# Layer norm statistics of the attention output: ScalarE sums and squares with GpSimd, in place of VectorE's batch-norm instructions

## What is computed

```python
attn = jax.nn.softmax(A1, axis=-1) - lamb * jax.nn.softmax(A2, axis=-1)
out = jnp.einsum('bhqk,bhkd->bhqd', attn, V)
out = out.transpose(0, 2, 1, 3).reshape(B, S, DIM)
out = out @ Wo
mu = jnp.mean(out, axis=-1, keepdims=True)
var = jnp.var(out, axis=-1, keepdims=True)
out = (out - mu) * jax.lax.rsqrt(var + LN_EPS) * gamma + beta
```

## Time and profile before

| what | value |
|---|---|
| median of 3 runs | 3935.44 us (3934.48 to 3940.17) |
| the profiled execution | 3935.01 us |
| its span, first to last instruction | 3933.2 us |
| mean granted TensorE clock | 0.981 of full speed |
| TensorE busy | 3720.3 us (95%) |
| VectorE busy | 3152.2 us (80%) |
| ScalarE busy | 2786.4 us (71%) |
| GpSimd busy | 1550.2 us (39%) |

### The profile page before, as it was taken

How to read it: one execution, slowest core, us unless ns; L and a number is a source line. 1 busy time by engine, 2 the same in 40 slices (tenths; PEclk the granted TensorE clock), 3 DMA queues, 4 the chain that set the end, 5 groups by cost and what they waited for, 6 DMA issues and landing times. The chain is left out here.

```text
span 3933.2 us, 63904 instructions
## 1 busy us (share of the span) xinstructions
PE 3720.3 (95%) x23714; PEld 1464.6 (37%) x23714; DVE 3152.2 (80%) x5433; ACT 2786.4 (71%) x3257; POOL 1550.2 (39%) x2057
## 2 busy tenths in 40 slices
PE   7997999999999999999999999999999879899999
PEld 5664222222222222222222222222222245588888
DVE  6776899999989999998999999899999433345454
ACT  4343888888888888887888788888888946522221
POOL 2320353263235325333532543253344357763330
PEclk9998999999999999999999999999999989899999
DMA  8775111111111111111101111110112069732220
GB/s 298 269 265 186 33 39 42 50 33 34 58 33 39 34 57 33 34 52 34 44 28 52 39 39 33 47 49 28 44 38 83 33 237 327 231 118 87 74 86 22
DMA packets 224553, 330.85 MB, mean 84 GB/s; under 512 B 29281, under 2 KB 165092, under 8 KB 219636
## 3 DMA queue, kind: packets, MB, share of 16 engines
q1 hardware_dynamic: 205812, 276.40, 21.3%
q0 software_dynamic: 18432, 50.36, 3.8%
HBM read 169.27 MB, written 156.34 MB: 83 GB/s over the span
## 5 line engine op out<-in xcount | busy, mean ns | idle before, releaser
L1734 DVE TENSOR_REDUCE first_rows<-psum 128x1 f32<-128x512 f32 x4000 | 2509.4, 684 | 173.1 <-PE psum L185 157.5
L1579 ACT ACTIVATE arena<-psum,exp_scale 128x1024 f32<-128x1024 f32 x2048 | 2159.8, 1111 | 275.8 <-PE psum L1439 269.8
L1455 PE MATMUL psum<-arena 128*32 128x512 f32 x8200 | 1107.5, 612 | 1.2 <-ACT arena L1579 0.6
L1619 POOL TENSOR_TENSOR arena<-arena 128x16 f32<-128x16 f32 x129 | 376.9, 2922 | 1504.0 <-ACT arena L1545 1504.0
L185 PE MATMUL psum<-arena 48*128 48x512 f16 x2048 | 649.6, 391 | 51.1 <-DVE first_rows L1734 22.8
L185 PE MATMUL psum<-first_rows 48*128 48x512 f16 x2048 | 622.7, 386 | 36.7 <-ACT arena L1539 7.7
L185 PEld LDWEIGHTS psum<-arena 48*128 48x128 f16 x2048 | 157.8, 93 | 865.2 <-DVE first_rows L1734 721.1
L185 PEld LDWEIGHTS psum<-first_rows 48*128 48x128 f16 x2048 | 154.9, 92 | 836.8 <-DVE first_rows L1734 715.1
L1439 PE MATMUL psum<-arena 50*128 50x512 f16 x2048 | 444.8, 382 | 11.6 <-ACT arena L1579 8.5
L1439 PE MATMUL psum<-first_rows 50*128 50x512 f16 x2048 | 447.3, 384 | 6.9 <-DMA first_rows<-arena 3.0
L1136 ACT ACTIVATE mix_arena<-psum,mix_arena 128x1024 f32<-128x1024 f32 x64 | 71.4, 1115 | 327.1 <-DVE mix_arena L1156 327.1
(11 more groups left out here) (186 smaller groups left out, 3944.0 us busy)
## 6 DMA issues: line engine op xcount, KB each, us to landing
scratch_split<-route_arena SPq DMA_DIRECT2D x64, 512.0 KB, 3.2
scratch_sorted_x<-route_arena SPq DMA_DIRECT2D x60, 512.0 KB, 4.7
scratch_sorted_y<-leaf_arena SPq DMA_DIRECT2D x60, 512.0 KB, 3.9
first_rows<-scratch_split SPq DMA_DIRECT2D x384, 64.0 KB, 2.2
arena<-scratch_split SPq DMA_DIRECT2D x384, 64.0 KB, 2.2
leaf_arena<-scratch_sorted_x SPq DMA_DIRECT2D x44, 512.0 KB, 5.8
leaf_start<-in_leafw SPq DMA_DIRECT2D x2, 5128.0 KB, 17.6
arena<-in_x SPq DMA_DIRECT2D x18, 512.0 KB, 4.9
```

The lines of the kernel that those rows point to most:

```text
L1455: last = nc.tensor.matmul(value_bank[32 * j:32 * j + 32, :], vaug[:, batch % 2, kt, 2 * pair + j % 2, :], prob[:, step % 2, j, :], start=k ...
L1579: nc.scalar.activation(prob[:, step % 2, 2 * h:2 * h + 2, :], score[:, 2 * h:2 * h + 2, :], ACT.Exp, scale=exp_scale[:, s % 2, s // 2:s // ...
L1619: nc.gpsimd.tensor_tensor(linv[:, c], total, minus_one, ALU.pow).then_inc(ochain, 1)
L1734: nc.vector.tensor_reduce(halfmax[:, odd, 2 * m + h, qt, c:c + 1], aux_bank[bank], AX.X, ALU.max).then_inc(bank_used[bank], 1)
```

## The change

The projections are read with an identity that also sums each row. GpSimd makes the negative mean of it (`mean`), in set 0 for group 0 and in set 1 for group 1. ScalarE squares the centred rows with a sum (`square`), one tile at the end of each of the steps 1 to 4 of set 1 (group 0) and set 2 (group 1); the squares themselves go to a buffer that is free by then. GpSimd makes the variance from the sum at the head of `inverse_std`, and `finish` adds the negative mean. VectorE's statistics go away.

```diff
--- before.py
+++ after.py
@@ -1588,6 +1588,8 @@
                                 act.wait_ge(extra_full, extras_before(k) + 1)
                                 read(i, s, kind, number, k % AUX)
                             k += 1
+                        if s in (1, 2) and 1 <= step <= OutputGroup.G:
+                            groups[s - 1].square(nc, act, i, step - 1)
 
             for i in range(BATCH):
                 body(i, i == LAST)
@@ -1599,6 +1601,9 @@
                     read_o(1, BATCH * 2 * PER_BATCH, k % AUX)
                 else:
                     read_group(BATCH, kind, number, k % AUX)
+            for h in range(2):
+                for q in range(OutputGroup.G):
+                    groups[h].square(nc, act, BATCH, q)
 
         @block.gpsimd
         def _(pool):
@@ -1672,6 +1677,9 @@
                         pool.wait_ge(extra_full, extras_before(group_end(i, 0, "turn")) + 1)
                     wait_read(pool, place(i, s, 11, "o", 0))
                     join_maps(2 * n + 1, s, 0)
+                    if s in (0, 1):
+                        wait_read(pool, group_end(i, s, "out"))
+                        groups[s].mean(nc)
                     if s in (1, 2):
                         groups[s - 1].inverse_std(nc, pool, i)
                         groups[s - 1].finish(nc, pool, nc.gpsimd, i)
@@ -1689,6 +1697,9 @@
                 body(i, i == LAST)
             wait_read(pool, START[BATCH] + EPILOGUE.index(("o", 1)))
             join_maps(BATCH * 2 * PER_BATCH, PER_BATCH - 1, 1)
+            for h in range(2):
+                wait_read(pool, START[BATCH] + EPILOGUE.index((f"out{h}", 3)))
+                groups[h].mean(nc)
             for h in range(2):
                 groups[h].inverse_std(nc, pool, BATCH)
 
@@ -1758,16 +1769,9 @@
                                     wait_read(dve, k)
                                     join_max(target % 2, i * PER_BATCH + target)
                             k += 1
-                        for h in range(2):
-                            if (s, step) == (1, 1 if h == 0 else 14):
-                                wait_read(dve, group_end(i, h, "out"))
-                                groups[h].stats(nc, link)
 
             for i in range(BATCH):
                 body(i, i == LAST)
-            for h in range(2):
-                wait_read(dve, START[BATCH] + EPILOGUE.index((f"out{h}", 3)))
-                groups[h].stats(nc, link)
             for h in range(2):
                 groups[h].finish(nc, dve, nc.vector, BATCH)
 
@@ -1792,7 +1796,7 @@
 
     G = 4
     LINKS = 2
-    POOL_LINKS = 9
+    POOL_LINKS = 10
 
     def __init__(self, nc, ctx, ar, consts, prefix):
         G = self.G
@@ -1800,15 +1804,14 @@
         self.sum_in = ar.take(G, DIM)
         self.oT = ar.take(G, KC, P)
         self.y = ar.take(G, DIM)
-        self.bn = ar.take(G, 6)
-        self.mv = ar.take(G, 2)
+        self.total, self.nmean, self.squares = ar.take(G), ar.take(G), ar.take(G)
         self.var, self.power, self.rstd, self.tmp = ar.take(G), ar.take(G), ar.take(G), ar.take(G)
 
         def sem(name):
             return ctx.enter_context(nc.semaphore(prefix + name))
 
         self.sum_ready, self.stored = sem("sum_ready"), sem("stored")
-        self.var_ready = sem("var_ready")
+        self.nmean_ready, self.squared = sem("nmean_ready"), sem("squared")
         self.pchain, self.y_ready = sem("group_pchain"), sem("y_ready")
 
     def tokens(self, a, g):
@@ -1839,44 +1842,47 @@
         return nc.scalar.activation(self.oT[:, 2 * q:2 * q + 2].rearrange("p q a b -> p (q a b)"), bank, ACT.Copy)
 
     def read_projected(self, nc, bank, q):
-        return nc.scalar.activation(self.y[:, q], bank[:, 0:DIM], ACT.Copy)
-
-    def stats(self, nc, link):
-        for q in range(self.G):
-            ins = nc.vector.bn_stats(self.bn[:, q], self.y[:, q])
-        link(ins)
-        for q in range(self.G):
-            ins = nc.vector.bn_aggr(self.mv[:, q], self.bn[:, q])
-        link(ins)
-        nc.vector.tensor_scalar(self.var, self.mv[:, :, 1], LN_EPS, None, ALU.add).then_inc(self.var_ready, 1)
+        return nc.scalar.activation(self.y[:, q], bank[:, 0:DIM], ACT.Identity, accum_out=self.total[:, q:q + 1])
+
+    def square(self, nc, act, n, q):
+
+        act.wait_ge(self.nmean_ready, n + 1)
+        nc.scalar.activation(self.oT[:, q].rearrange("p a b -> p (a b)"), self.y[:, q], ACT.Square, bias=self.nmean[:, q:q + 1],
+                             accum_out=self.squares[:, q:q + 1]).then_inc(self.squared, 1)
+
+    def mean(self, nc):
+
+        nc.gpsimd.tensor_scalar(self.nmean, self.total, -1.0 / DIM, None, ALU.mult).then_inc(self.nmean_ready, 1)
 
     def inverse_std(self, nc, pool, n):
 
         done = n * self.POOL_LINKS
-        pool.wait_ge(self.var_ready, n + 1)
+        pool.wait_ge(self.squared, (n + 1) * self.G)
+        nc.gpsimd.tensor_scalar(self.var, self.squares, 1.0 / DIM, LN_EPS, ALU.mult, ALU.add).then_inc(self.pchain, 1)
+        pool.wait_ge(self.pchain, done + 1)
         nc.gpsimd.tensor_tensor(self.rstd, self.var, self.power, ALU.pow).then_inc(self.pchain, 1)
-        pool.wait_ge(self.pchain, done + 1)
+        pool.wait_ge(self.pchain, done + 2)
         nc.gpsimd.tensor_tensor(self.tmp, self.rstd, self.rstd, ALU.mult).then_inc(self.pchain, 1)
-        pool.wait_ge(self.pchain, done + 2)
+        pool.wait_ge(self.pchain, done + 3)
         nc.gpsimd.tensor_tensor(self.tmp, self.tmp, self.var, ALU.mult).then_inc(self.pchain, 1)
-        pool.wait_ge(self.pchain, done + 3)
+        pool.wait_ge(self.pchain, done + 4)
         nc.gpsimd.tensor_scalar(self.tmp, self.tmp, -0.5, 1.5, ALU.mult, ALU.add).then_inc(self.pchain, 1)
-        pool.wait_ge(self.pchain, done + 4)
+        pool.wait_ge(self.pchain, done + 5)
         nc.gpsimd.tensor_tensor(self.rstd, self.rstd, self.tmp, ALU.mult).then_inc(self.pchain, 1)
 
     def finish(self, nc, eng, ops, n):
 
         done = n * self.POOL_LINKS
         wide = [P, self.G, DIM]
-        eng.wait_ge(self.pchain, done + 5)
-        ops.tensor_tensor(self.y, self.y, self.mv[:, :, 0:1].to_broadcast(wide), ALU.subtract).then_inc(self.pchain, 1)
         eng.wait_ge(self.pchain, done + 6)
+        ops.tensor_tensor(self.y, self.y, self.nmean.unsqueeze(2).to_broadcast(wide), ALU.add).then_inc(self.pchain, 1)
+        eng.wait_ge(self.pchain, done + 7)
         ops.tensor_tensor(self.y, self.y, self.rstd.unsqueeze(2).to_broadcast(wide), ALU.mult).then_inc(self.pchain, 1)
-        eng.wait_ge(self.pchain, done + 7)
+        eng.wait_ge(self.pchain, done + 8)
         ops.tensor_tensor(self.y, self.y, self.consts.gamma.unsqueeze(1).to_broadcast(wide), ALU.mult).then_inc(self.pchain, 1)
-        eng.wait_ge(self.pchain, done + 8)
+        eng.wait_ge(self.pchain, done + 9)
         ops.tensor_tensor(self.y, self.y, self.consts.beta.unsqueeze(1).to_broadcast(wide), ALU.add).then_inc(self.pchain, 1)
-        eng.wait_ge(self.pchain, done + 9)
+        eng.wait_ge(self.pchain, done + 10)
         eng.wait_ge(self.sum_ready, n * 16 + 16)
         ops.tensor_tensor(self.y, self.y, self.sum_in, ALU.add).then_inc(self.y_ready, 1)
 
```

## The result

The changed kernel takes 3885.62 us (median of 4 runs, 3881.76 to 3886.74) where the kernel before takes 3935.35 (4 runs, 3934.48 to 3940.17): a ratio of 0.9874 [0.9862, 0.9887], 1.26% faster, 49.7 us less. The forecast was 3895.5: the right direction, and 9.9 us too little, just outside the lower end of the range.

The account below looks back on a forecast made before the run. The prediction took VectorE's row maxima to bound the attention stage, with the statistics standing in VectorE's queue. Its sum: 3935.4 - 50.4 + 6.4 + 0 + 0 + 4.1 = 3895.5 us, range 3886 to 3922.

Parts of the forecast that it names:

- The statistics, -50.4: Attention loop: without VectorE's statistics the 16 three-step windows fall to plain steps, -50.4 us; at the least -29.3.
- its first rival: Loop: the stall goes, but TensorE still runs at 1.2 GHz there; only 29.3 us come back, 3917 us; chance 0.06.
- 21.1 us: Loop: the part of the statistics' 50.4 us put down to TensorE's slow clock behind the stall.
- The accumulator read in the projection, +6.4: Loop's projection steps: ScalarE's extra read releases the bank 0.10 us later, lengthening each step: +6.4 us, between 0 and 18.
- the ring: Projection step: projection, ScalarE's read, then TensorE's row product waiting for that read; a release 0.10 us later lengthens it by 0.10.
- The end of the stage, +4.1: End of attention: last squares, GpSimd's longer chain and the finishes are not hidden, +4.1 us, between +2.9 and +6.
- The squares, 0: Loop, four steps per group: ScalarE's 2.58 us in a 2.49 us step is covered by idle time: 0, at most 13 us.
- GpSimd, 0: Loop: a mean per group and one more inverse-deviation operation, about 0.3 us each, hold up nothing: 0.
- Another function table: Square steps: squares lie in another table, two loads for every square, +170 us, about 4070 us; chance 0.04.
- The clock part stays: Loop: ScalarE's backlog leaves TensorE short pauses and the 1.2 GHz clock; only 29.3 us come back, 3917 us; chance 0.06.
- Nothing changes: Loop: some other wait fills the same place, for example exponentials behind a late mean; about 3938 us; chance 0.04.
- ScalarE becomes the bound: Square and projection steps: nothing overlaps in square steps and accumulator reads cost their whole length; 3922 us; chance 0.10.

Follow-up runs that it names:

- Experiment 1: The kernel before without VectorE's statistics inside the loop and nothing in their place (groups there normalised with mean 0, variance 1): 3881.75 us, 0.9869.
- experiment 2: The changed kernel with VectorE's statistics put back at their two places in the loop, result not used: 3938.83 us, 1.0018.
- experiment 3: The kernel before with each group's statistics left on VectorE but spread over five steps, one tile per step: 3901.97 us, 0.9921.
- Experiments 4 and 5: The changed kernel with an unused copy behind each projection read, which then releases the bank: 64 columns (4), 3891.26 us; 256 columns (5), 3902.18 us.
- experiment 6: The changed kernel with every square inside the loop made twice, the second into a spare buffer: 3904.46 us, 0.993.
- experiment 7: The changed kernel with VectorE making mean and variance again in the epilogue, in place of the squares there: 3882.69 us, 0.9875.

## Why the prediction was right or wrong

**The statistics, -50.4: right**, in sum and in parts. The 16 windows fell to 119.74 us. Experiment 1 removes nothing else and gets -50.7 in the loop (2766.39 to 2715.72); experiment 2 puts the statistics back and loses the gain. That the slow clock goes with the pause, which the forecast assumed and its first rival doubted, is shown from the other side by experiment 3. That the sum was hit within 0.3 us is in part luck: where the clock falls differs from one execution to the next (experiment 2), and the forecast took its 21.1 us from the very execution that it is compared with.

**The accumulator read in the projection, +6.4: the step that failed.** The forecast said that "a release 0.10 us later therefore lengthens each such step by 0.10". The release did come later, by the 0.09 us that the mix stage had shown. But the step from a late weight load to a late matmul was not in the rows: in the kernel before the load is released 0.12 us ahead of its matmul, which keeps its 0.21 us behind the score matmul whether the load starts 0.09 or 0.18 us behind it. The forecast named this as the lower bound ("TensorE may be busy until then anyway") and took the middle. The earlier trace rows show the weight load alone; the two matmul rows beside it, 1148.09 and 1148.30, were there to be read. Experiments 4 and 5 show the ring that the forecast described, one accumulator read further on: 5.6 and 16.3 us. Made from the profiled execution, as the forecast says, its sum is 3935.0 - 50.4 + 6.4 + 4.1 = 3895.1, and the changed kernel's profiled execution took 3885.74: of the 9.4 us between them, this term is 6.4.

**The end of the stage, +4.1: right in mechanism, mis-sized by 2.4**; it measured +1.7. From the last read to the second finish's end 18.6 us were forecast and 17.4 measured. The squares follow each other at 0.49 us, not 0.57, and the second chain on GpSimd takes 6.55 us (3114.60 to 3121.15), not 7.4. A further 1.15 us is no step of the forecast: before, TensorE reached the last projections at a mean clock of 0.81, now at 1.00, so that the last read stands 15.4 us behind the last exponential instead of 16.6. The windows, before:

```profile
3152.40:3161.30 8.90, 6.33 (x24) 5.11 (x24) 1.99 (x10) 2.73 (x6) 3.43 (x10) 0.81 0.00 0
```

and after:

```profile
3102.30:3110.00 7.70, 4.76 (x24) 3.81 (x24) 0.00 (x0) 3.08 (x13) 1.85 (x6) 1.00 0.00 0
```

As far as the runs show, this part is luck: the changed end of stage does not decide it. With the same instructions there, experiment 6 had the slow clock again, and its last read stands 17.1 us behind the last exponential:

```profile
3120.48:3129.88 9.40, 6.44 (x24) 5.00 (x24) 0.00 (x0) 3.09 (x13) 1.85 (x6) 0.82 0.00 0
```

Experiments 2 and 4 had it too (16.7 us both), and so had experiment 3 with the statistics at the end (17.0); experiments 1, 5 and 7 ran at 1.00 (15.4, 15.7 and 15.4). Why it falls in some executions wasn't tried. Counted from the last read on, where no matmul takes part, the end of the stage grew by 17.4 - 14.6 = 2.8 us, next to the forecast's least of 2.9.

**The squares, 0: right, for a better reason than was given.** The forecast had 2.58 us of ScalarE in a step of 2.49 and covered the 0.09 with idle time. It added the accumulator read with its whole 0.19; it takes 0.09 from start to start (the square 0.40 against the forecast's 0.38), and the step comes to 2.50. Nothing was left over to cover, and nothing was left free: experiment 6 pays for the second square in full.

**GpSimd, 0: right.** The mean of the group shown is made at 1102.37 and its first square runs at 1112.87, ten microseconds later, as forecast. Its idle time before the next join fell from 5.93 to 2.30 us: 3.63, against the 3.6 that the forecast allowed.

```profile
1102.37 0.23 POOL L1855 TENSOR_SCALAR arena<-arena 128x4 f32<-128x4 f32 x1
...
1168.61 2.94 POOL L1624 TENSOR_TENSOR arena<-arena 128x16 f32<-128x16 f32 x1 [2.30 <-ACT arena L1545]
```

**The rivals.** *Another function table* fell: one load in the trace, and no square waits. *The clock part stays* fell: 1.00 in every window. *Nothing changes* fell by the result, and experiment 1 says why. *ScalarE becomes the bound* is true in a form that costs nothing: in square steps it is now as full as VectorE. The rule beside that rival, of the Trainium skill in "ScalarE: Activation LUTs", Rules for kernel authors, sends simple arithmetic to VectorE and not to ScalarE; its reason is a speed for bf16 in a fast mode, where the tiles here are f32. Taken by itself it speaks against this change, which gained 49.7 us, because VectorE's queue was the one that TensorE waited for, while ScalarE's new work lay in its gaps. At the end of the stage, where VectorE has nothing else to do, experiment 7 agrees with the rule, by 2.8 us.

**The range** had its lower end at 3886. With the terms as measured (the statistics -50.7 and the additions +0.2, both by experiment 1) the forecast's sum is 3935.4 - 50.7 + 0.2 + 1.7 = 3886.6; the last microsecond lies where the change does nothing (0.4 ahead of the loop, -0.9 behind the leaf stage's start) and in the spread of the runs. What kept the low end so close was +2.9 as the least for the end of the stage, where no room was left for an earlier last read. With the slow clock there, as before, the same sum is about 1.15 us more: that the time came to lie outside the range hangs on that chance. Two of the signs that the forecast named did not come: no projection step is 0.1 us longer, and the leaf stage begins 48.4 us earlier (3179.40 to 3131.03) where 35 to 40 were expected.

## What to carry to other kernels

A block of work on the engine that the others wait for costs more than its length when TensorE's clock falls behind the pause that it makes: here 16 blocks of 1.92 us, 31 us, cost 50, and cutting each block into five gave 32 of these back. The clock did not fall behind every such block: 3 of the 16 windows kept 1.00. Before pricing a later release, read the start of the instruction that needs the result and not only that of its weight load: between the two lay 0.12 us, and that decided 6 us. Price a small instruction by the distance from its start to its neighbour's, not by its record, which overlaps.

## What the runs showed of the hardware

- ScalarE's accumulator read has a record of 0.19 to 0.24 us; an instruction that has nothing to wait for starts 0.09 us behind its start (1113.27 and 1113.36). The weight load that waits for it came 0.09 us later than behind the plain copy (0.18 instead of 0.09 us behind the score matmul).
- A square and an exponential run behind the same table load: 72 squares among 2048 exponentials, one load of 1283 ns.
- An engine that a window shows as busy for 7.46 of 7.46 us can still have slack: records of neighbours overlap, and VectorE's four maxima take 2.37 us (experiment 3) in a step of 2.49.
- VectorE and GpSimd can hold each other up in both directions. Beside VectorE's wide operations GpSimd's small operation takes 1.23 us instead of 0.20 (3114.60 and 3112.07, the same line of the kernel), and beside GpSimd's wide operation VectorE's addition on four columns took 0.80 us instead of 0.17 (experiment 2), while the other instructions of the statistics kept their lengths. The Trainium skill, "GPSIMD Engine Reference", section 1, says that the two share SBUF interfaces and contend when VectorE's instruction has two SBUF inputs or runs in a two-port mode. GpSimd's 1.23 us stand beside such an instruction, VectorE's finish with two inputs, and agree. VectorE's 0.80 us belong to an instruction with one input; in what mode it ran no row here shows.
